# Two-layer transformer kernel: attention regrouped from single heads to groups of four

## The reference, cut to what matters

```python
q = (hidden_states @ q_proj_w.T).reshape(b, s, H, Q_DIM).transpose(0, 2, 1, 3)
compressed = hidden_states @ kv_a_proj_w.T
...
kv = _rmsnorm(k_pass_lat, kv_a_ln_w) @ kv_b_proj_w.T          # rank 64 latent -> keys and values
...
scores = jnp.einsum('bhqd,bhkd->bhqk', q, k) * scaling
scores = jnp.where(causal[None, None], scores, NEG)
probs = jax.nn.softmax(scores.astype(jnp.float32), axis=-1).astype(q.dtype)
out = jnp.einsum('bhqk,bhkd->bhqd', probs, v)
out = out.transpose(0, 2, 1, 3).reshape(b, s, H * V_DIM)
return out @ o_proj_w.T
```

## Time and profile before

| what | value |
|---|---|
| median of 3 runs | 997.33 us (988.61 to 999.35) |
| span of the profiled execution | 985.5 us (its time with what lies around it was not recorded; the median is 11.8 us more) |
| mean granted TensorE clock | 0.932 |
| TensorE busy | 850.1 us, 86% |
| VectorE busy | 452.2 us, 46% |
| ScalarE busy | 322.4 us, 33% |
| GpSimd busy | 261.2 us, 27% |
| attention stage, from first scores to the residual of the last tile | 82.7 to 472.7 us |
| VectorE groups L894, L899, L903 | 31.3, 21.3, 36.3 us |

### The profile page before, as it was taken

How to read it: one execution, slowest core, us unless ns; L and a number is a source line. 1 busy time by engine, 2 the same in 40 slices (tenths; PEclk the granted TensorE clock), 3 DMA queues, 4 the chain that set the end, 5 groups by cost and what they waited for, 6 DMA issues and landing times.

```text
span 985.5 us, 17100 instructions
## 1 busy us (share of the span) xinstructions
PE 850.1 (86%) x5125; PEld 700.9 (71%) x5126; DVE 452.2 (46%) x1231; ACT 322.4 (33%) x768; POOL 261.2 (27%) x432
## 2 busy tenths in 40 slices
PE   5999998999999999998279993476888799999964
PEld 4778886788999888887179992466866555556653
DVE  4123664647475665664334442466755122222244
ACT  1233554654554444443024341121232022222210
POOL 2003535242414132134300003777306000000241
PEclk9997999999999999998589997698989999999988
DMA  6339401010001000001569994556352111111111
GB/s 172 83 93 415 149 1 43 7 39 12 32 2 43 2 26 18 2 27 60 204 209 352 355 358 131 177 171 212 125 171 80 33 43 43 43 43 32 49 59 38
DMA packets 83856, 102.20 MB, mean 104 GB/s; under 512 B 16096, under 2 KB 74464, under 8 KB 82528
## 3 DMA queue, kind: packets, MB, share of 16 engines
q1 hardware_dynamic: 64112, 69.20, 21.7%
q0 software_dynamic: 7680, 20.98, 6.5%
q10 hardware_dynamic: 12016, 11.41, 3.4%
HBM read 67.22 MB, written 34.34 MB: 103 GB/s over the span
## 4 chain that ended last, share of the span: by engine, by line
PE 33%; POOL 7%; issue 5%; DVE 3%; DMA 2%; ACT 0%; POOLq 0%; SPq 0%; DVEq 0%; ACTq 0%
PE scores L1634 9%; POOL area L569 6%; PE scores L1484 5%; PE acc_ps L1654 4%; PE probsT_ps L1598 3%; PE scores L1495 2%; PE scores L1287 2%; PE probsT_ps L1473 1%; PE scores L1288 1%; PE scores L1289 1%; DMA area<-xe_d 1%; PE probsT_ps L1644 1%; POOL rstd L517 1%; POOL xe_d L525 1%; PE misc_ps L1619 1%
## 5 line engine op out<-in xcount | busy, mean ns | idle before, releaser
L1384 PE MATMUL misc_ps<-area 128*128 128x65 f32 x1152 | 152.5, 278 | 4.7 <-DVE ctx_n L903 1.6
L1384 PEld LDWEIGHTS misc_ps<-area 128*128 128x128 f32 x1152 | 146.5, 196 | 11.0 <-ACT area L649 2.5
L887 DVE TENSOR_REDUCE neg_max<-scores 128x1 f32<-128x128 f32 (+7 forms) x128 | 96.8, 756 | 67.6 <-PE scores L1358 64.8
L511 POOL TENSOR_TENSOR q_lo<-area,q_hi 128x128 fp32r<-128x128 f32 x128 | 59.1, 461 | 179.7 <-ACT q_hi L668 171.4
L649 ACT COPY area<-probsT_ps 128x512 f32<-128x512 f32 (+3 forms) x128 | 64.9, 507 | 120.0 <-PE probsT_ps L1368 115.4
L643 ACT ACTIVATE area<-scores,neg_max 128x128 f32<-128x128 f32 (+7 forms) x128 | 95.7, 747 | 0.0
L1368 PE MATMUL probsT_ps<-ident,area 128*128 128x128 f32 x576 | 91.0, 281 | 2.1 <-ACT ctxT L653 1.8
L1634 PE MATMUL scores<-area 128*128 x184 | 86.7, 615 | 4.0 <-issue 2.9
L1287 PE MATMUL scores<-kT_hi,q_hi 128*128 128x512 f32 (+3 forms) x192 | 77.3, 402 | 6.3 <-POOL q_lo L511 4.8
L1368 PEld LDWEIGHTS probsT_ps<-ident,area 128*128 128x128 f32 x576 | 69.1, 149 | 7.6 <-ACT ctxT L653 6.9
L569 POOL DMA_INDIRECT area<-ye_d,fetch_now x64 | 63.9, 999 | 23.5 <-issue 18.5
(11 more groups left out here) (217 smaller groups left out, 1496.4 us busy)
## 6 DMA issues: line engine op xcount, KB each, us to landing
area<-gate_up SPq DMA_DIRECT2D x32, 384.0 KB, 6.9
xe_d<-area SPq DMA_DIRECT2D x8, 1024.0 KB, 10.3
area<-w SPq DMA_DIRECT2D x8, 1024.0 KB
area<-xe_d SPq DMA_DIRECT2D x32, 256.0 KB, 7.0
ye_d<-area ACTq DMA_DIRECT2D x32, 256.0 KB, 5.9
area<-down SPq DMA_DIRECT2D x32, 192.0 KB, 7.1
area<-w SPq DMA_DIRECT2D x8, 512.0 KB, 7.9
area<-xd_d SPq DMA_DIRECT2D x23, 128.0 KB, 2.2
```

What stands on the lines that cost most here:

```text
L887: dve.tensor_reduce(neg_max[:, u:u + 1], banks[u][:, 0:(qt + 1) * P], AX.X, ALU.max, negate=True).then_inc(max_ready, 1)
L1384: last = pe.matmul(ctx_ps, probsT[:, u, k * P:(k + 1) * P], latent[:, k, :], start=k == 0, stop=k == qt)
```

## The change

Heads are taken in groups of four (`QUAD`); a tile has 4 groups, the stage 32. A group's four rows of exponentials are kept (`prob_rows`, 10 rows). For each key block the four heads' blocks are transposed into one PSUM bank of 512 columns. ScalarE rounds them from PSUM to `pT_hi`, VectorE subtracts that from PSUM to `pT_lo`. `latent` now holds the rounded half (64 columns) and the rest (64 columns) of the latent keys and is stationary; `pT_hi` and `pT_lo` move, so the context of four heads comes out transposed, 128 rows (both halves) by 512. ScalarE copies it, and one matmul per head with `wvo`, which now holds the head's matrix twice, one under the other, gives that head's output. VectorE multiplies it by the head's inverted row sum and adds it to `x1`, starting from the input. The row sum comes from the exponential's accumulated output. Query splits are made on GpSimd, two heads at once, in three buffers. A slot `(G, i)` handles the scores of head `4G+i+2`, some of the blocks of group `G-1` and the output of head `i` of group `G-2`. All loops over pairs are written out. The small products of routing use the other half of the bank that the output uses. The ring's first expert weights wait for the last transposes, as the kept rows lie in their place.

```diff
+QUAD = 4
+SETS = HEADS // QUAD
+GROUPS = TILES * SETS
+ROWS_KEPT = 10
...
+        prob_rows = [area2[:, 2048 + 1024 * m:3072 + 1024 * m] for m in range(6)] + [
+            area4[:, 1024 + 1024 * m:2048 + 1024 * m] for m in range(ROWS_KEPT - 6)]
...
+        ctx_ps = misc
+        out_ps = acc[:, 0:HID]
+        x1T_ps = acc[:, HID:2 * HID]
+        place_ps = acc[:, HID:HID + E0]
+        logits_ps = acc[:, HID:HID + E0]
...
+        def steps_at(G, place):
+            if not 0 <= G < GROUPS:
+                return []
+            n = tile_of(G) + 1
+            return [k for k in range(n + 1) if k * 8 // (n + 1) == place]
...
+        def head_slots(body):
+            for G in range(GROUPS + 2):
+                for i in range(QUAD):
+                    body(G, i, QUAD * G + i)
...
             sp.wait_ge(zeroed, 16 * ZEROINGS)
+            sp.wait_ge(pT_ps, blocks_to(GROUPS))
             for e in range(0, RING, 2):
                 load_weights(e, e)
...
+            def split_q(m):
+                qt, h = divmod(2 * m, HEADS)
+                two = qT[:, h * T:(h + 2) * T].rearrange("p (h t) -> p h t", h=2)[:, :, qt * P:(qt + 1) * P]
+                if m >= 3:
+                    pool.wait_ge(scores_ready, 2 * (m - 3) + 2)
+                pool.tensor_copy(q_his[m % 3], two).then_inc(q_half, 1)
+                pool.wait_ge(q_half, m + 1)
+                pool.tensor_tensor(q_los[m % 3], two, q_his[m % 3].bitcast(f32), ALU.subtract).then_inc(q_split, 1)
...
+                act.activation(row_of(n)[:, 0:L], banks[u][:, 0:L], ACT.Exp, bias=neg_max[:, u:u + 1],
+                               accum_out=rsum[:, s, k:k + 1]).then_inc(probs_ready, 1)
...
+            def copy_hi(b):
+                act.wait_ge(pT_ps, b + 1)
+                if b >= 2:
+                    act.wait_ge(ctx_step, b - 1)
+                act.activation(pT_hi[b % 2], pT[b % 2][:], ACT.Copy).then_inc(hi_done, 1)
...
+            def act_slot(G, i, n):
+                for place in (2 * i, 2 * i + 1):
+                    for k in steps_at(G - 1, place):
+                        if k <= tile_of(G - 1):
+                            copy_hi(blocks_to(G - 1) + k)
+                if i == QUAD - 1 and 0 <= G - 1 < GROUPS:
+                    copy_ctx(G - 1)
+                if n + 2 < TILES * HEADS:
+                    exp_probs(n + 2)
+                if G >= SETS + 2 and G % SETS == 2 and i == 2:
+                    copy_x1T(tile_of(G) - 1)
...
+            def copy_lo(b):
+                dve.wait_ge(pT_ps, b + 1)
+                dve.wait_ge(hi_done, b + 1)
+                dve.tensor_tensor(pT_lo[b % 2], pT[b % 2][:], pT_hi[b % 2].bitcast(f32), ALU.subtract).then_inc(lo_done, 1)
...
+            def add_head(n):
+                t, h = divmod(n, HEADS)
+                s, k = stat_of(n)
+                dve.wait_ge(out_ready, n + 1)
...
+                dve.scalar_tensor_tensor(x1[:, t, :], out_ps, rinv[:, s, k:k + 1], x1[:, t, :] if h else x_in[:, t, :],
+                                         ALU.mult, ALU.add).then_inc(out_read, 1)
...
+            def dve_slot(G, i, n):
+                for k in steps_at(G - 1, 2 * i):
+                    if k <= tile_of(G - 1):
+                        copy_lo(blocks_to(G - 1) + k)
+                if n + 2 < TILES * HEADS:
+                    row_max(n + 2)
+                for k in steps_at(G - 1, 2 * i + 1):
+                    if k <= tile_of(G - 1):
+                        copy_lo(blocks_to(G - 1) + k)
+                if i == 1 and 0 <= G - 1 < GROUPS:
+                    invert(G - 1)
+                t = tile_of(G) - 1
+                if t >= 0 and (G % SETS, i) == (2, 3):
+                    read_logits(t)
+                if t >= 0 and (G % SETS, i) == (3, 1):
+                    read_place(t)
+                if 0 <= G - 2 < GROUPS:
+                    add_head(QUAD * (G - 2) + i)
+                if t < 0:
+                    return
+                if (G % SETS, i) == (1, QUAD - 1):
+                    attention_variance(t)
+                if (G % SETS, i) == (2, 0):
+                    finish_tile(t)
+                if (G % SETS, i) == (2, QUAD - 1):
+                    choose(t)
+                if G % SETS == 3 and i in (1, 2):
+                    next(places[t])
...
+            def context(G, k):
+                b = blocks_to(G) + k
+                pe.wait_ge(hi_done, b + 1)
...
+                pe.matmul(ctx_ps[:], latent[:, k, :], pT_hi[b % 2], start=k == 0, stop=False)
+                pe.wait_ge(lo_done, b + 1)
+                pe.matmul(ctx_ps[:], latent[:, k, :], pT_lo[b % 2], start=False, stop=k == tile_of(G)).then_inc(ctx_step, 1)
+
+            def output(n):
+                G, i = divmod(n, QUAD)
+                pe.wait_ge(ctx_copied, G + 1)
+                if n:
+                    pe.wait_ge(out_read, n)
+                h = n % HEADS
+                pe.matmul(out_ps, ctxT[:, G % 2, i * P:(i + 1) * P], wvo[:, h * HID:(h + 1) * HID],
+                          start=True, stop=True).then_inc(out_ready, 1)
...
             pe.wait_ge(qT_done, HEADS)
+            scores(0)
+            scores(1)
...
+            def pe_slot(G, i, n):
+                t = tile_of(G) - 1
+                g = G % SETS
+                if t >= 0 and (g, i) in ((2, 2), (2, 3), (3, 1)):
+                    pe.wait_ge(out_read, QUAD * (G - 2) + i)
+                    if (g, i) == (2, 2):
+                        transpose_x1(t)
+                    elif (g, i) == (2, 3):
+                        route(t)
                     else:
+                        count_places(t)
+                steps(G - 1, 2 * i)
+                if n + 2 < TILES * HEADS:
+                    scores(n + 2)
+                steps(G - 1, 2 * i + 1)
+                if 0 <= G - 2 < GROUPS:
+                    if t >= 0 and (g, i) == (2, 2):
+                        pe.wait_ge(x1T_done, t + 1)
+                    if t >= 0 and (g, i) == (2, 3):
+                        pe.wait_ge(logits_read, t + 1)
+                    if t >= 0 and (g, i) == (3, 1):
+                        pe.wait_ge(place_read, t + 1)
+                    output(QUAD * (G - 2) + i)
```

More of the change, by code:

```diff
@@ L517, in rstd_of, with send @@
                 pool.tensor_tensor(rstd[:, s:s + 1], mv[:, s, 1:2], minus_half[:, 0:1], ALU.pow).then_inc(rstd_done, 1)
[L519 to L521 removed]
+            def send(t, k):
                 pool.wait_ge(send_done, t + 1)
[L524 to L526 removed]
@@ L560, in fetch @@
+            head_slots(pool_slot)
+            for k in range(TOP0):
+                send(TILES - 1, k)
             def fetch(t, u, first, behind):
@@ new lines, in _ @@
+            places = [assign(t) for t in range(TILES)]
+            def dve_slot(G, i, n):
[26 more added lines that the diff above has]
+                    next(places[t])
@@ L1019, in _ @@
+            head_slots(dve_slot)
             finish_tile(TILES - 1)
@@ L1022, in _ @@
             read_place(TILES - 1)
-            for part in assign(TILES - 1):
+            for part in places[TILES - 1]:
                 pass
@@ L1359, in scores @@
                 last.then_inc(scores_ready, 1)
-            def transpose_probs(qt, n, u, m=None):
-                pe.wait_ge(probs_ready, n + 1)
-                for c in range(chunks(qt)):
-                    if m is not None and c == 1:
-                        pe.wait_ge(ctxT_done, m)
-                    bank = pT[u if chunks(qt) == 1 else c]
-                    for k in range(4 * c, min(qt + 1, 4 * c + 4)):
-                        last = pe.transpose(bank[:, (k % 4) * P:(k % 4 + 1) * P], probs[:, u, k * P:(k + 1) * P],
-                                            ident[:])
-                    last.then_inc(pT_ps[c], 1)
@@ L1388, in transpose_ctx, with transpose_probs @@
[L1388 to L1396 removed]
+            def transpose_probs(G, k):
+                b = blocks_to(G) + k
+                pe.wait_ge(probs_ready, QUAD * (G + 1))
+                if b >= 2:
+                    pe.wait_ge(hi_done, b - 1)
+                    pe.wait_ge(lo_done, b - 1)
+                for i in range(QUAD):
+                    last = pe.transpose(pT[b % 2][:, i * P:(i + 1) * P], row_of(QUAD * G + i)[:, k * P:(k + 1) * P],
+                                        ident[:])
+                last.then_inc(pT_ps, 1)
```

387 lines of the change are left out of this document (109 added, 278 removed).

## The result

The changed kernel takes 1054.29 us (median of 4 runs, 1046.88 to 1057.71) against 996.48 us of before, measured beside it. The ratio is 1.0567, 95% interval 1.0505 to 1.063: slower, by 57.8 us in the medians. The forecast was +34 (1031, range 976 to 1058).

The account below looks back on a forecast made before the run. TensorE was taken to bound the attention before the change. Afterwards 344+7+3.4+14+56 = 424 us against 390, +34, gave a span of 1019.5 and, with the 11.8 offset kept, 1031 us; range 976 to 1058.

Parts of the forecast that it names:

- The term that turned the sign: Attention slots with routing: TensorE waits for additions and readers in the shared output bank, 8 us a tile, 56 in all.
- a stage of 368: Attention without the routing waits: 344+7+3.4+14 = 368 us, 22 less than the 390 before.
- a steady group 12.35: Four heads of tile 4 without routing, worked out slot by slot: 12.35 us, of which 10.7 is TensorE's own work.
- The rival's sign: A steady group of tile 4 under 11.2 us would show TensorE still the bound, 973 us; chance 0.2.
- The forecast's bound: Limits set on the routing waits in the attention: 0 if they fall into existing stalls, and 70 us.
- The clock rival: Attention, tiles from 1 on: one more low-clock stretch each, about 3.4 us, 24 us more, 1055 us; chance 0.15.
- the end of the stage: Tile 7 at 68.8 us, and the drain after the last scores at 18 less 4, so 14.
- the grouping: Attention in groups of four heads: 344 us for the tiles, plus 7 for low clock at the start and 14 drain.
- 37 us less TensorE work: Attention on TensorE: context 61 us less, output 31 more, context transposes 7 less.
- The rival in which TensorE stays the bound: Attention: rounding and subtraction run ahead, routing waits fall into them; 24 us less, 973; chance 0.2.
- the start, +3.4: First scores wait for the last q copy and a double split on POOL: 86.2 instead of 82.8 us, +3.4.
- the ring of expert weights: Loads of 2.3 MB moved behind the last transposes, 6.3 us; costed at nothing, 6 us without cover.

## Why the prediction was right and wrong

**Right: the sign and its mechanism.** The term that turned the sign was routing inside the attention, at 56 us above a stage of 368. The runs: 365.8 without routing, and idle time 51 us less. The way it was argued (small matmuls waiting for the addition, the next output for a reader that stands behind maximum and exponential) is what the order of time at 270 to 276 shows. In tile 4 the interval with the routing slots was 19.47 us against 12.79, 10.44 and 13.3 for the other three groups, 7.3 over their mean (forecast 3.1+1.6+2.6 = 7.3 in those slots, a steady group 12.35). Tiles 4, 5 and 6 with their routing came to 56.0, 63.1 and 66.0, where 49.4, 53.5 and 61 with 8 for each were forecast. That agreement is luck in part. Without routing the four groups of tile 4 take 10.57, 10.40, 12.02 and 12.08 us, 45.1 and not 49.4; so routing costs this tile 10.9 (the forecast's own terms, 7.3+1.4, add up to 8.7, and it took 8), and the neighbours that 19.47 was held against carry a part of it. The rival's sign, a steady group under 11.2, was missed by little: the mean is 11.3.

**Mis-sized: routing, 56 against 74 to 81** (66 between chips of the faster kind). The forecast's bound was 70. The idle part was right: 51. Two parts were lacking. One is the clock: 30 to 52 us less of it low without routing, at the estimated 0.31 us each 9 to 16 us. The forecast held routing to stalls at full clock and put the clock into a rival of its own with 24 us and a chance of 0.15. It was a part of the same case: low clock in the attention is 66.8 and 44.4 us against 28.3 and 18.0. The other is the small products' own time. The forecast's 368 was added up from groups without them, and its 56 from waits alone; TensorE's busy time in the attention is 7 us less when their records are left out. A rest of 5 to 6 us, in part the chip's, stays open. The clock rival's 1055 is the number nearest to the measured 1054, but by a coincidence of sizes: from before to the changed kernel the low clock grew by 26 to 38 us, at 0.31 each 8 to 12 and not 24.

**Mis-sized: the end of the stage.** Drain and tile 7 were put at 68.8+14, and up to 10 for routing: 93. They took 106.4. Of it 33.6 us lie between the last scores and the last addition, 26.4 in the run without routing: the blocks of the last group wait for rounding and subtraction with no scores left to fill in, and the clock is low in parts of it too (516.7 to 520.1, and from 523.5 on). Tiles 2 and 3 were 9 us over as well (45.3+52.5 against 42+46.5).

**Right in sum, half wrong in its parts: the grouping.** The stage without routing was forecast at 344+7+14 = 365 us from the first scores on, and 365.8 were measured. It is luck in part: tile 4 was 4.3 us faster than forecast, and the last tile with its drain took 90.2 against 83. Nor is it a gain of 22: the 390 beside it holds the old kernel's routing, and without it that stage takes 364.6. "37 us less TensorE work" was worked out from unhindered distances. Between the two kernels without routing it is 18.5. The 0.12 us a block that products behind a wait lose, 17.6 us, would account for nearly all that is missing; in the run without routing the pair and its successor's start take 713 ns as well. The rival in which TensorE stays the bound (973) failed by this and by the routing, not by VectorE's load: VectorE is busy 286 us, 64% of the stage, where 297 and over 70% were expected.

**Wrong: the start, +3.4.** First scores were at 82.3 and not 86.2. The forecast went by the splits of q and missed that `wvo` held twice makes the value product wider, which saves 0.30 us a head.

**Right at nothing: the ring of expert weights.** The one long wait for loads behind the attention is 18.4 us in both kernels, for rows of x1 (L1426, L1473 before).

**The offset.** Span and median were joined by 11.8 us, since the profiled execution of before was a fast one. The profiled run of the changed kernel took 1053.47 us, 1.8 over its span. That is why spans differ by 66.2 and medians by 57.8.

**Open: what stands behind the attention.** Its length follows the chip. With routing in place, the old order has 507.0 us there on a chip where the kernel before took 974 and 512.8 and 515.7 where it took 992 to 996; the versions of the new order have 507.3 to 512.9 on the first kind and 519.5 to 526.9 on the second. So the change adds 0 to 14 us by these single traces, 3.8 in the two that were taken on one chip. What it adds there, and why the chips differ, no run tells.

**Open: what lowers the clock.** The Trainium skill (TensorE: Matmul & The Clock Gate, A second HAM failure mode: psum-queue depth-cycling) says that short idle times between groups of matmuls that cycle through PSUM make it swing. The runs lean to that: idle and low clock in the attention are 5.8 and 6.8 us, 25.5 and 14.3, 44.1 and 23.5, 76.8 and 65.2, 76.7 and 66.8. But 78.0 went with 44.4 in the same kernel. Two stretches of it, first in the one trace, then in the other:

```profile
210.00:219.70 9.70, 6.44 (x35) 4.51 (x35) 6.08 (x14) 4.83 (x12) 4.84 (x7) 1.00 0.09 29
219.70:230.00 10.30, 8.81 (x27) 6.18 (x27) 4.29 (x14) 2.06 (x5) 2.11 (x3) 0.50 0.04 13
```

```profile
210.00:219.70 9.70, 6.15 (x31) 4.32 (x32) 5.21 (x11) 3.69 (x9) 4.02 (x6) 0.98 0.09 29
219.70:230.00 10.30, 7.97 (x39) 5.46 (x39) 5.07 (x16) 3.35 (x7) 2.35 (x4) 0.85 0.04 13
```

TensorE was busy for 6.44 of 9.7 us in the first stretch in the one and 6.15 in the other; the low clock that followed lasted 10.3 us and 3.4.

## What to carry to other kernels

When small work shares a PSUM bank with a steady stream, price each of its steps by what stands ahead of its reader in the reader's queue, and set the reader where its engine last had nothing newer to wait for: moving three readers and three matmul groups, with no work removed, gave back more than four of six per cent. A saving in matmuls counts only where they don't start behind a wait. A block of slack at the product gave nothing while the bank's readers came late, and 2.4% once they did not; then the wait stood at the bank that is read, where slack was not tried. Before calling a grouping good or bad, take the interleaved work out of both kernels: here that showed a tie, where 368 without it against 390 with it had promised 22 us.

## What the hardware showed that I had not expected

- An fp32 product with 64 stationary columns delays what follows more than one with 128: 0.58 against 0.30 us to the next start, in the last 13 of the 16 heads (the first three run at low clock or between other waits), ratio 0.995.
- The exponential's accumulated sum is an instruction of its own on ScalarE, 0.19 us, 24.8 us in all for 128. It starts 0.1 us before the exponential ends, and the next instruction 0.1 before it ends (275.78 and 275.88 above), so it holds ScalarE for less than its 0.19. I had taken nothing. Whether it costs time here was not tried. In tiles 3 to 7:

```profile
L625 ACT ACTIVATION_READ_ACCUMULATOR area<-scores,neg_max 128x1 f32 x67 | 12.9, 193 | 0.0
```

- A wait costs TensorE more than its idle time shows: 0.12 us per block of two products, hidden in durations of 464 in place of 404 ns.
- Output and routing results lie in different halves of one bank and still had to take turns. The Trainium skill (PSUM — Partial Sum Buffer, PSUM bank collisions raise a hardware error) has the reason: two engines may not touch one bank in the same partitions at once, whichever columns they want. No run here tried it; what the runs show is the cost of taking turns, 9.6 us of output waits for the addition that fell to 0.2 with a second bank for 28 of the 128 outputs.
